# Top-38 search and layer norm on Trainium2: x's load spread over 33 quads, squares as tile products of TensorE, 59 second counts of ScalarE between its first ones

## What is computed

```
x = x + xattn(layernorm(x), ctx_4096, ...)       # layernorm over the last axis (2048)
k = 38                                           # of C = 64 channels
_, topk_idx = top_k(moveaxis(channel_map, 1, 2), k)      # channel_map = ctx_4096, 1601 rows
mask = zeros((B, L, C)).at[b_idx, l_idx, topk_idx].set(1.0)
```

## Time and profile before

| what | value |
|---|---|
| median of 3 runs | 2226.02 us (2225.61 to 2226.99) |
| the profiled execution: time, span | 2228.47 us, 2226.5 us |
| TensorE busy | 1926.3 us (87%) |
| VectorE busy | 1314.7 us (59%) |
| ScalarE busy | 1124.3 us (50%) |
| GpSimd busy | 1025.6 us (46%) |
| mean granted clock of TensorE, share of 2.4 GHz | 0.960 |
| DMA | 407.58 MB, mean 183 GB/s |

### The profile page before, as it was taken

How to read it: one execution, slowest core, us unless ns; L and a number is a source line. 1 busy time by engine, 2 the same in 40 slices (tenths; PEclk the granted TensorE clock), 3 DMA queues, 4 the chain that set the end, 5 groups by cost and what they waited for, 6 DMA issues and landing times. The chain is left out here.

```text
span 2226.5 us, 37959 instructions
## 1 busy us (share of the span) xinstructions
PE 1926.3 (87%) x14353; PEld 1554.5 (70%) x14353; DVE 1314.7 (59%) x2065; ACT 1124.3 (50%) x2527; POOL 1025.6 (46%) x911
## 2 busy tenths in 40 slices
PE   4677788777752648999999999999999999999999
PEld 4666666655640246788878888888878878788887
DVE  5999999999899988644435601244455326631111
ACT  7999998998956665433233422232323323422222
POOL 2222233332227505666555546556645445544554
PEclk9999999999885869999999999999999999999999
DMA  9999998999922025522235443222254355334443
GB/s 387 398 383 389 346 330 321 329 330 323 340 91 91 19 75 173 156 81 80 85 128 180 134 139 107 89 78 80 88 189 143 114 168 178 131 118 137 146 137 112
DMA packets 158390, 407.58 MB, mean 183 GB/s; under 512 B 15616, under 2 KB 44544, under 8 KB 156544
## 3 DMA queue, kind: packets, MB, share of 16 engines
q1 hardware_dynamic: 157920, 403.52, 51.6%
q0 software_dynamic: 288, 1.64, 0.2%
HBM read 379.93 MB, written 25.17 MB: 182 GB/s over the span
## 5 line engine op out<-in xcount | busy, mean ns | idle before, releaser
L1408 POOL TENSOR_TENSOR t<-t,t 128x512 fp32r<-128x512 f32 (+1 forms) x488 | 653.3, 1351 | 670.2 <-ACT t L1401 599.7
L1957 PE MATMUL ps<-t,t 128*128 128x512 f32 x1856 | 734.4, 396 | 14.8 <-POOL t L1408 9.4
L1959 PE MATMUL ps<-t,t 128*128 128x512 f32 x1856 | 723.4, 390 | 0.0
L1958 PE MATMUL ps<-t,t 128*128 128x512 f32 x1856 | 722.8, 389 | 0.0
L1401 ACT ACTIVATE t<-t 128x512 fp32r<-128x512 f32 (+1 forms) x488 | 293.7, 609 | 697.0 <-PE ps L1959 373.8
L786 PE MATMUL ps<-t,t 128*128 128x128 bf16 (+1 forms) x6097 | 420.4, 226 | 178.0 <-DVE t L471 169.3
L786 PEld LDWEIGHTS ps<-t,t 128*128 128x128 bf16 x6097 | 370.3, 102 | 265.7 <-DVE t L471 223.7
L471 DVE TENSOR_SCALAR t<-t,t 128x1601 bf16<-128x1601 f32 x469 | 480.5, 1054 | 14.2 <-PE ps L786 9.7
L699 ACT ACTIVATE t<-t,t 128x1601 bf16<-128x1601 f32 x256 | 417.0, 1629 | 33.5 <-DVE t L636 29.7
L1957 PEld LDWEIGHTS ps<-t,t 128*128 128x128 f32 x1856 | 348.4, 188 | 94.2 <-POOL t L1408 14.0
L1959 PEld LDWEIGHTS ps<-t,t 128*128 128x128 f32 x1856 | 348.4, 188 | 73.7
(11 more groups left out here) (240 smaller groups left out, 1796.7 us busy)
## 6 DMA issues: line engine op xcount, KB each, us to landing
t<-ctxT SPq DMA_DIRECT2D x256, 800.5 KB, 7.0
t<-wqkv SPq DMA_DIRECT2D x192, 256.0 KB, 3.1
t<-wo SPq DMA_DIRECT2D x128, 256.0 KB, 4.6
t<-wb SPq DMA_DIRECT2D x128, 256.0 KB, 3.6
t<-xT SPq DMA_DIRECT2D x48, 256.0 KB, 7.1
t<-x1d SPq DMA_DIRECT2D x32, 256.0 KB, 4.9
x2d<-t SPq DMA_DIRECT2D x32, 256.0 KB, 2.0
t<-x2d SPq DMA_DIRECT2D x8, 1024.0 KB, 7.2
```

Source lines behind the costliest of these rows:

```text
L1408: e.tensor_tensor(wlo[r][:, 0:nk, :], raw[r][:, 0:nk, :], wh[r][:, 0:nk, :].bitcast(F32), ALU.subtract).then_inc(w_lo, 1)
L1957: e.matmul(bank[:, :], wh[r][:, q, :], xl, start=(kt == 0), stop=False)
L1958: e.matmul(bank[:, :], wlo[r][:, q, :], xh, start=False, stop=False)
L1959: m = e.matmul(bank[:, :], wh[r][:, q, :], xh, start=False, stop=(c == NCH[p] - 1 and q == nk - 1))
```

## The change

x's tiles are loaded one per four context tiles instead of one per three, so over 33 quads. The steps of layer norm move to later quads. The squares are no longer ScalarE's: TensorE multiplies each centred tile by itself in four blocks of 128 columns, `x` as weights and as moving operand, and adds over the 16 tiles; the sums of squares are the diagonals of the four blocks, which VectorE picks out by a product with the identity and a reduction. The squares' buffer and the four turning products go. `by_act` now holds for all quads from 1 to 59, 16 more. ScalarE makes the second count of quad i-1 behind the second sign of quad i instead of behind the fourth, and in those quads the fourth slot's copy also moves behind the second sign. GpSimd decides it at the end of its iteration. VectorE's last three closing steps of a batch move from around L669 to behind the fourth to sixth mask, and the first maxima of a batch wait for less.

```diff
 def by_act(g):
-    return 1 <= g < NQ - 4 and not (25 <= g + 1 <= 56 and g % 2 == 0)
+    return 1 <= g < NQ - 4
...
-            if n >= 6 and n % 3 == 0 and (n - 6) // 3 < 2 * NT:
-                h, xt_ = (n - 6) // 3 // NT, (n - 6) // 3 % NT
+            if n >= 6 and (n - 6) % 4 == 0 and (n - 6) // 4 < 2 * NT:
+                h, xt_ = (n - 6) // 4 // NT, (n - 6) // 4 % NT
...
             if n == RID_TILE:
-                e.wait_ge(ln0_sqsum, 2 * NT)
+                e.wait_ge(set_up, 3)
...
-    LN0_SUM, LN0_MEAN, LN0_SUB, LN0_VAR = (15, 30), (23, 39), (24, 40), (43, 58)
+    LN0_SUM, LN0_MEAN, LN0_SUB, LN0_VAR = (19, 35), (27, 43), (28, 44), (45, 61)
...
-            x, j = XN[:, h, :, :], (i - LN0_SUB[h]) // 2
-            if LN0_SUB[h] <= i < LN0_SUB[h] + 16 and (i - LN0_SUB[h]) % 2 == 0:
+            x, d = XN[:, h, :, :], i - LN0_SUB[h]
+            if 0 <= d < 16 and d % 4 < 2:
+                j = 2 * (d // 4) + d % 4
...
-            if i == LN0_VAR[h] + 1:
-                e.wait_ge(ln0_turned, 2 * h + 1)
-                e.tensor_scalar(ln0_inv[h], ln0_sums[h][:, 0:4], 1.0 / L, EPS, ALU.mult, ALU.add).then_inc(ln0_var, 1)
+            if i == LN0_VAR[h]:
+                products = ln0_rs[h][:, :].rearrange("p (c n) -> p c n", n=128)
+                e.wait_ge(ln0_sqsum, h + 1)
+                e.wait_ge(ln0_sub, 8 * h + 8)
+                e.tensor_tensor(products, ln0_sums[h][:, :].rearrange("p (c n) -> p c n", n=128),
+                                ident.rearrange("p (a n) -> p a n", a=1).to_broadcast([128, 4, 128]), ALU.mult).then_inc(ln0_var, 1)
+                e.wait_ge(ln0_var, 4 * h + 1)
+                e.tensor_reduce(ln0_inv[h], products, AX.X, ALU.add).then_inc(ln0_var, 1)
+                e.wait_ge(ln0_var, 4 * h + 2)
+                e.tensor_scalar(ln0_inv[h], ln0_inv[h], 1.0 / L, EPS, ALU.mult, ALU.add).then_inc(ln0_var, 1)
...
-                e.activation(lsq[:, :], XN[:, h, t, :], ACT.Square).then_inc(ln0_sq, 1)
...
-                e.activation(ln0_rs[h][:, :], ln0_sums[h][:, :], ACT.Copy).then_inc(ln0_flat, 1)
...
-            t = i - LN0_SUB[h] - 2
-            if 0 <= t < NT and u == 0:
-                e.wait_ge(ln0_mean, h + 1)
-                e.wait_ge(ln0_sq, 16 * h + t + 1)
-                e.matmul(ln0_sums[h][:, :], ones, lsq[:, :], start=(t == 0), stop=(t == NT - 1)).then_inc(ln0_sqsum, 1)
...
+            t = i - LN0_SUB[h] - 1
+            if 0 <= t < NT:
+                if u == 0:
+                    e.wait_ge(ln0_mean, h + 1)
+                    e.wait_ge(ln0_sub, 8 * h + t // 2 + 1)
+                x = XN[:, h, t, 128 * u:128 * u + 128]
+                m = e.matmul(ln0_sums[h][:, 128 * u:128 * u + 128], x, x, start=(t == 0 and u == 0), stop=(t == NT - 1 and u == 3))
...
                 if half == 0 and b >= 2 and t0 == 0:
-                    e.wait_ge(fin, NF * (b - 1))
+                    e.wait_ge(fin, NF * (b - 2) + 7)
+                    e.wait_ge(tied, 4 * (b - 1))
...
-                end_batch([] if first_steps else [7])
                 w = insB[:, 4 * c:4 * c + 4]
                 e.copy_predicated(vc[:, :, 0], w, vc[:, :, 2]).then_inc(b_set, 1)
-                end_batch([] if first_steps else [8, 9])
...
+                if not first_steps and k in (3, 4, 5):
+                    end_batch([k + 4])
...
-        if u == 0 and by_act(i - 2):
-            e.wait_ge(b_signed, ACT_NO[i - 2] + 1)
+        if u == 2 and by_act(i - 1):
+            e.wait_ge(b_signed, ACT_NO[i - 1] + 1)
...
-        e.wait_ge(signed, 4 * g + 8)
+        e.wait_ge(signed, 4 * g + 6)
...
-                if u == 0 and 2 <= i:
+                if u == by_act(i - 2) and 2 <= i:
                     counts_scalar(e, i - 1, 3)
-                if 1 <= i <= NQ + 1:
-                    for v in {2: [0], 3: [1]}.get(u, []):
-                        counts_scalar(e, i, v)
-            if by_act(i - 1):
-                sign_b_scalar(e, i - 1)
+                if u == 1 and by_act(i - 1):
+                    sign_b_scalar(e, i - 1)
+                if 2 <= u and 1 <= i <= NQ + 1:
+                    counts_scalar(e, i, u - 2)
...
-            if by_act(i - 2):
-                decide_b_gpsimd(e, i - 2)
             copy_gpsimd(e, 4 * i)
...
+            if by_act(i - 1):
+                decide_b_gpsimd(e, i - 1)
```

More of the change, by code:

```diff
@@ L570, in ln0_scalar @@
                 e.activation(Mn[:, :], ln0_sums[h][:, :], ACT.Copy, scale=1.0 / L).then_inc(ln0_mean, 1)
-            t = i - LN0_SUB[h] - 1
-            if 0 <= t < NT:
-                e.wait_ge(ln0_sub, 8 * h + t // 2 + 1)
-                if 16 * h + t:
-                    e.wait_ge(ln0_sqsum, 16 * h + t)
-                else:
-                    e.wait_ge(set_up, 3)
-                e.activation(lsq[:, :], XN[:, h, t, :], ACT.Square).then_inc(ln0_sq, 1)
-            if i == LN0_VAR[h]:
-                e.wait_ge(ln0_sqsum, 16 * h + 16)
-                if h:
-                    e.wait_ge(ln0_sub, 16)
-                e.activation(ln0_rs[h][:, :], ln0_sums[h][:, :], ACT.Copy).then_inc(ln0_flat, 1)
             if i == LN0_VAR[h] + 1:
-                e.wait_ge(ln0_var, 2 * h + 1)
+                e.wait_ge(ln0_var, 4 * h + 3)
                 e.activation(ln0_inv[h], ln0_inv[h], ACT.Sqrt).then_inc(ln0_std, 1)
             if i == LN0_VAR[h] + 2:
-                e.wait_ge(ln0_var, 2 * h + 2)
+                e.wait_ge(ln0_var, 4 * h + 4)
                 for c in range(4):
@@ L591, in ln0_scalar @@
             if i == LN0_VAR[h] + 3:
-                e.wait_ge(ln0_turned, 2 * h + 2)
+                e.wait_ge(ln0_turned, h + 1)
                 e.activation(ln0_rs[h][:, :], ln0_sums[h][:, :], ACT.Copy).then_inc(ln0_rstd, 1)
@@ L602, in ln0_tensor @@
                     m.then_inc(ln0_total, 1)
-            t = i - LN0_SUB[h] - 2
-            if 0 <= t < NT and u == 0:
-                e.wait_ge(ln0_mean, h + 1)
-                e.wait_ge(ln0_sq, 16 * h + t + 1)
-                e.matmul(ln0_sums[h][:, :], ones, lsq[:, :], start=(t == 0), stop=(t == NT - 1)).then_inc(ln0_sqsum, 1)
-            if i == LN0_VAR[h] + 1 and u == 0:
-                e.wait_ge(ln0_flat, 5 * h + 1)
-                for c in range(4):
-                    m = e.matmul(ln0_sums[h][:, c:c + 1], ln0_rs[h][:, 128 * c:128 * c + 128], ident[:, 0:1], start=True, stop=True)
-                m.then_inc(ln0_turned, 1)
+            t = i - LN0_SUB[h] - 1
[5 more added lines that the diff above has]
+                m = e.matmul(ln0_sums[h][:, 128 * u:128 * u + 128], x, x, start=(t == 0 and u == 0), stop=(t == NT - 1 and u == 3))
+                if t == NT - 1 and u == 3:
+                    m.then_inc(ln0_sqsum, 1)
             if i == LN0_VAR[h] + 3 and u == 0:
-                e.wait_ge(ln0_flat, 5 * h + 5)
+                e.wait_ge(ln0_flat, 4 * h + 4)
                 e.matmul(ln0_sums[h][:, :], ones, ln0_rs[h][:, :], start=True, stop=True).then_inc(ln0_turned, 1)
@@ L820, in ln0_out @@
         e.wait_ge(ln0_rstd, h + 1)
-        e.wait_ge(ln0_sq, 16 * h + 16)
         e.tensor_tensor(x, x, bc(ln0_rs[h][:, :], tiles), ALU.mult).then_inc(signal, 1)
```

## The result

The changed kernel takes **2240.5 us** as the median of five runs (2235.6 to 2244.4), against 2226.0 us before: a ratio of 1.006, 95% interval 1.0042 to 1.0077. It is slower by 14.5 us. The forecast was 2228.9 us with a range of 2217 to 2237, so the time lies outside of it, on its slow side.

The account below looks back on a forecast made before the run. The prediction took ScalarE to bound quads 4 to 23 and VectorE quads 24 to 59 before the change. Its terms, -0.7 + 8.3 - 4.5 - 0.2 = +2.9 us on 2226.0, gave 2228.9 us, range 2217 to 2237.

Parts of the forecast that it names:

- the period: ScalarE's time per plain quad, quads 4 to 59: 9.28 us plus 0.42 for touching counts and copies, 9.70 us.
- Rival 1: Touching pairs on ScalarE cost nothing, its period stays 9.28 us: -7.6 us in all, 2218.4 us; chance 0.26.
- VectorE at 37.1 us per four quads: VectorE's work in four search quads, against ScalarE's 38.8 us, so ScalarE becomes the bound.
- Rival 3: VectorE stays the bound in quads 24 to 59 at 10.04 us a quad: +7.4 us, 2233.4 us; chance 0.10.
- the new wait: VectorE waits some 1.6 us at L487 in each batch's first closing quad, priced at 0.13 us a quad.
- the statistics: First half's layer norm statistics, from quad 45: 1.0 us through VectorE plus 2.5 on ScalarE, together 3.5 us.
- I price a fall at 0.9: TensorE clock falls in closing quads: 0.9 us each, two in the 5 early quads, one in the 9 later.
- column sums: Added cost where sums meet other work: 0.35 us in quad 22; 0.65 + 0.65 + 0.35 in quads 38, 42, 26.
- the tail: From quad 60 on: second half's statistics and less VectorE idle time, net -0.2 us (bounds -3 and +3).
- whose pause the new products partly fill: Layer norm's new TensorE products partly fill the later closing quads' pause, so only one clock fall was counted in nine.
- The cover: The second count ahead of ScalarE's copy covered 1.6 us before; without it, whatever delays TensorE there shows.
- rival 2: TensorE's clock drops in nearly all 14 closing quads, 0.9 us each: +9.9 us, 2238.8 us; chance 0.18.

Follow-up runs that it names:

- e3: Changed kernel with the third and fourth slots' copies behind the next quad's first and second signs, so counts and copies alternate: 2208.8 us.
- e1: Changed kernel with ScalarE's old order back (second count behind the fourth sign, fourth slot's copy behind the first, GpSimd deciding in the next iteration): 2203.0 us.
- e4: Changed kernel with 30 more products of 128x128, not needed for the result, on TensorE in each of the 14 closing quads: 2230.9 us.
- e10: e1 with the fourth slot's copy behind the second sign instead of the first in the 14 closing quads: 2223.3 us.
- e9: Kernel before with only VectorE's closing steps of a batch spread as in the changed kernel: 2216.3 us.
- e7: e1 with 43 second counts on ScalarE as before; products on TensorE, x loads and closing steps as changed: 2215.8 us.
- e2: Changed kernel with only the fourth slot's copy back behind the first sign: 2227.3 us.
- e6: Kernel before with all 59 second counts on ScalarE at their old place, squares still on ScalarE: 2229.3 us.
- e8: e1 with VectorE's closing steps of a batch back at their old places: 2207.8 us.

## Why the prediction was wrong

**Right: the period.** 9.28 + 0.42 = 9.70; the plain quads take 9.71 from start to end of the search, and the copies that touch stand 0.44 apart. e3 confirms the reason: with the neighbours parted the same work takes 9.31. Rival 1 was wrong. Behind it stood the Trainium skill's statement that back-to-back ACTIVATEs overlap by 93 ns ("ScalarE: Activation LUTs", "What ACT_TABLE_LOAD costs"). It doesn't hold for neighbours of which one waits for the other: in the earlier trace rows the second count of such a pair starts 1.82 us behind one of 1.63.

**Right, as far as can be seen: VectorE at 37.1 us per four quads**, and ScalarE as the bound. e1, at 9.28 us a quad (37.12 for four), shows both engines about level: VectorE is busy 329.05 of 339.88 us in the middle, 36.6 per four; it waits 6.6 us for copies in all, ScalarE 1.1 for maxima. Rival 3 was wrong.

**Right: the place and size of the new wait.** 1.6 us at L487 in 14 quads forecast, 22.6/14 = 1.61 measured. Its own price, 0.13 us a quad, came out as 0.18 (quads 34 and 50: 9.88 and 9.89).

**Right: the statistics.** Quads 45 to 48 cost 1.25 + 1.32 + 0.96 + 0.28 = 3.8 us over 9.70, against 3.5 counted.

**Wrong: "I price a fall at 0.9 ... and count two in the 5 early quads and one in the 9 later ones".** The granted clock fell in 11 of the 14, all but quads 34, 46 and 50. In quads 6, 10 and 18 the clock was low already when VectorE stopped at L487 (from 66.55, 107.51 and 186.02 us), and quads 13, 17 and 29 have a fall without any such wait; so not every fall is this pause's. Two of the 11 (quads 6 and 18) cost nothing, in the other nine the quad takes 0.8 to 2.0 us more than 9.70. Over 9.70 the early closing quads lost 0.18, 0.78, 1.00, 0.22 and 1.95, together 4.1 us, against 2.8 counted; the later ones without quad 46 lost 9.8, against 3.75 counted for wait, fall and column sums. These 7.3 us are most of the 10.3 by which the spans' difference (+13.2) exceeds the +2.9. The rest: the remaining early quads 0.5, the remaining middle ones 0.5, the statistics 0.3, the tail, which cost 1.0 and not -0.2, and the start, which gave 0.4 and not 0.7. e4 shows the cause of the large term: with the same wait and without the falls from quad 22 on, 9.6 us are gone. What the wait costs at full clock is seen in quads 34 and 50, 0.18 each, 2.5 us for 14.

The reasons given for so few falls failed as well. **"whose pause the new products partly fill"**: in quad 54 one pair of products of 0.47 us stands ahead of a pause that is still 1.82 us, and the clock falls. They stand at fixed places between the counts and not in the gap. **Where sums meet a fall** the two were added at full clock: 0.35 for a column sum. In quads 22, 26, 38 and 42, which hold column sums, ScalarE waits 1.84 to 2.04 us. In e4 these four take 10.0 to 10.2 us; at 1.2 GHz a pair of sums takes 2.05 and not 1.10 us (e10's quad 22), and stands between two late counts. The cover, which the prediction held to be what the new order loses, doesn't decide it either: e10 has it, and there the late copy costs 20.3 us. So the price of a fall isn't one number; it depends on what TensorE has to do until the quad's last count.

**Right in kind, with too small a chance: rival 2**, the falls in nearly all closing quads, 2238.8 us with 0.18. The measured time is 1.7 us above it. That it is so near is partly luck: rival 2 had 14 closing quads at 0.9, and there were nine that cost something, at 1.5 us on average. The evidence of the earlier trace rows spoke for it: ahead of that fall TensorE had paused for 1.41 and 0.45 us, and the new pause was to be longer than either and to come in 14 quads. Against it stood only that it had not yet happened in most of them. The range, which should have held most of that rival's spread, ended 1.8 us below its mean.

**What no run of before could show, and the sum did not ask:** against what the change is to be measured. The prediction compared 9.70 with VectorE's 10.04 and booked a gain. e1 shows that the same relief of VectorE gives 9.44 us a quad in the middle (339.88/36, the statistics among it). The 0.42 us per quad were a loss there too, only one that the comparison with before hid.

## The ledger

Each kernel's median is taken against that of the kernel before on its own chip (-10.4 for e9, -11.4 for e7, -23.9 for e1, +0.4 for e2, +4.0 for e4, +14.5 for the changed kernel), and a step is the difference of two of them. Most medians are uncertain by 2 to 4 us.

| step | kernel | change, us |
|---|---|---|
| closing steps spread | e9 | -10.4 |
| products on TensorE, x loads | e7 | -1.0 |
| 16 more second counts | e1 | -12.5 |
| touching pairs | e2 | +24.3 |
| late copy: the wait by itself | e4 | +3.6 |
| late copy: TensorE's clock | changed kernel | +10.5 |

The last is 9.6 when the two medians are compared directly, as above. Which of the first three rows a gain is booked in depends on the order in which they are taken. The counts alone (e6, +2.1) are worth nothing and the products alone next to nothing (-1.0), but both together, without the spread closing steps, give 19.4 us (e8): With the squares still on ScalarE a quad with the count takes 9.80 us (e6), without them 9.28. The spread closing steps are worth 10.4 us in the kernel before and 4.5 on top of e8, where that difference is not clear of the noise.

## What to carry to other kernels

When a change makes an engine pause that feeds TensorE, ask of every such pause whether TensorE's clock fell behind one like it, and if so count the fall in all of them, priced by the work that TensorE has left until someone waits for it. On an engine that sets the pace, order its instructions so that dependent ones don't touch, and so that whatever another engine's chain needs goes first; a copy of 0.26 us in the wrong place cost 13 to 20 us here, though in e3, at the same place but with VectorE coming later, it did not. So ask when the waiting engine gets there, not only when the copy is made. And when a change bundles several edits, compare each with the kernel that has the others, not with the kernel before: e1 beats both (2203.0 against 2226.9 us) and differs from the losing one by the order of one loop.

## What the runs showed that was not expected

Idle-filling work paid: 420 products that nobody needs (14 times 30) made two kernels faster, by 9.6 and 5.9 us, though they take TensorE 1.84 us each time.

Three steps of 1.3, 0.25 and 0.16 us, placed between later masks instead of ahead of the second, gained 10.4 us in the kernel before. There the clock was low in ten of the 14 quads behind a batch's first closing steps; with the steps spread it was in one of them.

What a fall costs depends on slack: e2 has eight falls in quads 5 to 19 that cost nothing, while in the changed kernel those in quads 10 and 14 cost 0.8 and 1.0 us. Why some pauses of about 1.9 us are followed by a fall and others are not (quad 50 had 1.96 us at L779 and kept its clock, quad 54 had 1.82 and lost it) stays open:

```profile
514.86 0.88 PE L779 MATMUL ps<-t,t 128*128 128x128 bf16 x13 [1.96 <-DVE t L471]
```
